# Delta net: first units in the second stage's end, softmax subtraction on GpSimd, z ahead of the first T, tail on two engines

## The reference

```python
x = x + L0_xattn(norm(x), ctx)   # 16 heads over 128 context rows, softmax
x = x + L0_attn(norm(x))         # 16 heads, scores * tril mask, softmax(scores / 8)
x = x + L0_ffn(norm(x))          # Hadamard transforms around a gated MLP of 1024
x = x + L1_xattn(norm(x), ctx)   # 16 heads, causal mask, softmax
x = x + L1_attn(norm(x))         # gated delta net, 16 key heads, 32 value heads
x = x + L1_ffn(norm(x))          # 32 experts, top 8
```

```python
state = state * exp(g_t); delta = (v_t - k_t @ state) * beta_t
state = state + outer(k_t, delta); out_t = q_t @ state
o = out * rsqrt(mean(out**2) + eps) * norm_w * silu(z)     # z: one more projection
```

## Time and profile before

| | us |
|---|---|
| runs shown, median of 3 | 1669.58 (1667.72 to 1670.84) |
| the profiled execution's own time | 1666.14 |
| its span | 1664.3 |
| TensorE busy | 1547.2 (93%) |
| VectorE busy | 1130.2 (68%) |
| ScalarE busy | 598.3 (36%) |
| GpSimd busy | 553.9 (33%) |
| stage 1 | 0 to about 190 |
| stage 2 | about 193 to 520 |
| stage 3 | about 521 to 1398 |
| stage 4 | about 1399 to 1664 |

### The profile page before, as it was taken

One profiled execution on the slowest core, in us unless ns is written; L12 is line 12 of the kernel. 1 busy time (PEld: TensorE's weight loads), 2 busy tenths in 40 slices (PEclk: granted clock), 3 DMA queues, 4 the chain that ended last, 5 costly groups with the idle time before them and its releaser, 6 DMA issues. The chain is left out here.

```text
span 1664.3 us, 34006 instructions
## 1 busy us (share of the span) xinstructions
PE 1547.2 (93%) x14224; PEld 1084.9 (65%) x14224; DVE 1130.2 (68%) x1745; ACT 598.3 (36%) x1038; POOL 553.9 (33%) x885
## 2 busy tenths in 40 slices
PE   7999679979996698999999999999999996999999
PEld 3444358867883366777777777767777784565556
DVE  4666487597675677788888888887788833543433
ACT  2223144345333334444444444444544531111110
POOL 1200052123211545556545465454564431000000
PEclk9999889989998799999999999999999997999999
DMA  7533300010000121121121221112211113200000
GB/s 217 159 90 91 76 1 1 25 28 1 1 1 7 30 42 35 42 56 47 37 52 42 47 50 48 37 46 43 55 46 34 43 27 151 84 1 0 13 1 13
DMA packets 150536, 75.76 MB, mean 46 GB/s; under 512 B 128304, under 2 KB 131632, under 8 KB 148592
## 3 DMA queue, kind: packets, MB, share of 16 engines
q1 hardware_dynamic: 150384, 73.60, 17.5%
HBM read 55.73 MB, written 17.83 MB: 44 GB/s over the span
## 5 line engine op out<-in xcount | busy, mean ns | idle before, releaser
L1719 DVE SCALAR_TENSOR_TENSOR acc<-PS,wc,acc 128x504 f32<-128x504 f32 (+2 forms) x384 | 281.4, 733 | 93.2 <-ACT acc L1452 84.1
L2004 PE MATMUL PS<-HT,wgu 128*128 128x512 f32 x384 | 173.8, 597 | 0.6 <-ACT HT L2050 0.6
L1452 ACT ACTIVATE acc<-PS,wc 128x512 f32<-128x512 f32 x128 | 87.8, 686 | 172.3 <-PE PS L1183 119.7
L1183 PE MATMUL PS<-HT,wv 128*128 128x512 f32 x256 | 128.6, 626 | 11.4 <-DVE acc L1719 11.4
L1729 DVE SCALAR_TENSOR_TENSOR y<-th,acc 128x512 f32<-128x512 f32 x128 | 115.9, 906 | 22.7 <-ACT th L1456 21.4
L1183 PE MATMUL PS<-HT,wkq 128*128 128x512 f32 x256 | 124.5, 610 | 6.6 <-DVE acc L1719 4.7
L1642 POOL TENSOR_TENSOR rr<-nm,con 128x16 f32<-128x16 f32 x16 | 46.8, 2927 | 241.1 <-DVE nm L1747 241.1
L1200 PE MATMUL PS<-wz,HT 128*128 128x256 f32 x512 | 125.1, 392 | 0.7 <-DMA wz<-in_gdn_w 0.7
L2004 PEld LDWEIGHTS PS<-HT,wgu 128*128 128x128 f32 x384 | 73.3, 192 | 74.8 <-issue 72.7
L2140 DVE SCALAR_TENSOR_TENSOR act<-th,PS 128x512 f32<-128x512 f32 x48 | 33.0, 687 | 127.2 <-ACT th L2064 127.2
L1346 PE MATMUL PS<-wo,ogT 128*128 128x256 f32 x512 | 115.3, 383 | 3.5 <-DVE dl L1782 2.4
(11 more groups left out here) (252 smaller groups left out, 3036.5 us busy)
## 6 DMA issues: line engine op xcount, KB each, us to landing
a_rows<-AT SPq DMA_DIRECT2D x16, 512.0 KB, 2.6
wk<-in_l0x_k SPq DMA_DIRECT2D x16, 384.0 KB, 3.6
wgu<-in_moe_gu SPq DMA_DIRECT2D x6, 1024.0 KB, 14.9
queries_scratch<-tts SPq DMA_DIRECT2D x32, 128.0 KB, 2.7
wkq<-in_gdn_w SPq DMA_DIRECT2D x16, 256.0 KB, 2.7
wv<-in_gdn_w SPq DMA_DIRECT2D x16, 256.0 KB, 2.7
wz<-in_gdn_w SPq DMA_DIRECT2D x16, 256.0 KB, 3.3
wo<-in_gdn_w SPq DMA_DIRECT2D x16, 256.0 KB, 3.0
```

The costliest lines, as they stand in the source:

```text
L1183: mm = pe.matmul(PS[:, QB[q], :], w[:, o:o + DK], HT[:, k, f * 512:(f + 1) * 512], start=(k == 0), stop=(k == DC - 1))
L1452: a.activation(acc[:, f, :], PS[:, QB[q], :], ACT.Copy, scale=wc[:, h % 2, 4 * c + 3:4 * c + 4]).then_inc(s["tap"], 1)
L1719: v.scalar_tensor_tensor(a0, p0, wc[:, h % 2, 4 * c + 2 - k:4 * c + 3 - k], a0, ALU.mult, ALU.add).then_inc(s["conv"], 1)
L2004: mm = pe.matmul(PS[:, 2 * (i % 2) + w, :], wgu[:, m, k, w, :], HT[:, k, f * N:(f + 1) * N], start=(k == 0), stop=(k == DC - 1))
```

## The change

1. `w_project`, `w_tap`, `w_tanh`, `w_conv`, `w_silu` and `w_ab` in phase2: the units q = 0, 2, 4 of head 0 (the first 512 tokens of k, q and v0) and the a/b projection of 7 of the 8 tiles are done at the end of stage 2. Their buffers lie over `kvT` and `W2`, which are no longer read then; `y` is now the two halves `yA` and `yB`. phase3 starts its counts at three units and takes the other units in the order 1, 3, 5, 6, 7.
2. The softmax subtraction of parts 1 and 3 moves from VectorE to GpSimd (`lower`). All four orders of phase2 are written anew.
3. phase3's start: a and b are turned into `ga` by GpSimd and VectorE, the z groups of head 0 and a step of its own, `first`, replace `step(0)`; z comes before the first T.
4. `factors`: the power in two halves of 8 columns, the half of k first; the half of q, `sk` and the square of q's half come after `Et`. For all heads.
5. The end of phase3: `sum_o` before `gate`, half of the last multiply and one of the last two copies on VectorE, the norms of phase4's first 4 tiles made around the last residual. The first 1 MB of phase4's weights (`wg0`) is loaded in phase3.

```diff
@@ phase2
-                load(1); load(0); load(2); load(3); load(4); load(5); load(6); load(7)
+                load(0); load(1); load(3); load(2); load(4); load(5); load(6); load(7)
+                def w_project(k):
+                    if k == 0:
+                        pe.wait_ge(s["hT0"], 8)
+                    elif k == 2:
+                        pe.wait_ge(s["w_conv"], 3)
...
+                def w_ab():
+                    for p in range(3):
+                        pe.wait_ge(s[f"hT{p}"], 8)
...
-                turn(4, 3); scores(7, 1); project_out(5, 1); turn_p(6, 1); values(6, 1); project_out(6, 1); turn(5, 3)
-                turn_p(7, 1); turn(6, 3); values(7, 1); project_out(7, 1); turn(7, 3)
...
+                project_out(5, 1); w_project(0); turn_p(6, 1); w_project(1); values(6, 1); w_project(2); project_out(6, 1)
+                turn_p(7, 1); values(7, 1); turn(5, 3); project_out(7, 1); turn(6, 3); w_ab(); turn(7, 3)
...
+                def lower(t, a):
+                    p, n = at(t)
+                    g.wait_ge(s[f"sm{p}"], n * 10 + a * 3 + 6)
+                    g.tensor_tensor(probs(p), probs(p), each(mx[:, p, :], S), ALU.subtract).then_inc(s[f"sm{p}"], 1)
...
-                    v.wait_ge(sem, at0 + 2)
-                    v.tensor_tensor(x, x, each(mx[:, p, :], S), ALU.subtract).then_inc(sem, 1)
...
+                mask_spread(7, 1); residual(5, 3); stats(5, 3); w_conv(0); sums(7, 1); w_conv(1); residual(6, 3)
+                w_silu(0); stats(6, 3); w_silu(1); apply(5, 3); apply(6, 3); w_conv(2); residual(7, 3); stats(7, 3)
+                w_silu(2); apply(7, 3)
@@ phase3, TensorE: the start, and first() in place of step(0)
+                project_ab()
                 project(0, 1)
-                project_ab()
-                for q in range(2, 5):
-                    project(0, q)
+                project(0, 3)
+                project(0, 5)
+                decay_sums(0)
                 scores(0)
-                decay_sums(0)
-                for q in range(5, NQ):
-                    project(0, q)
+                project(0, 6)
+                project_z(0, 0)
+                project(0, 7)
+                project_z(0, 1)
                 turn_v(0, 0)
+                def first():
+                    project(1, 0)
+                    turn_v(0, 1)
+                    project(1, 1)
+                    project_z(0, 2)
+                    decay_sums(1)
+                    project(1, 2)
+                    project_z(0, 3)
+                    project(1, 3)
+                    project(1, 4)
+                    cross(0, 4)
+                    scores(1)
+                    grow(0, 4)
+                    project(1, 5)
...
@@ phase3, GpSimd: factors
+                    g.tensor_tensor(rr[:, par, kh], nm[:, kh], C("mhalf")[:, kh], ALU.pow).then_inc(s["rr"], 1)
...
                         g.tensor_tensor(Et[:, hv, :, :], Ed[:, hv, :, :], over(C("upper"), TILES), ALU.mult).then_inc(s["et"], 1)
+                    g.tensor_tensor(rr[:, par, qh], nm[:, qh], C("mhalf")[:, qh], ALU.pow).then_inc(s["rr"], 1)
+                    g.tensor_tensor(sk[:, par, :], nm[:, kh], rr[:, par, kh], ALU.mult).then_inc(s["rr"], 1)
...
@@ phase3, ScalarE: swap_scale
-                    a.wait_ge(s["rr"], h * 5 + 3)
+                    a.wait_ge(s["rr"], h * 7 + 6)
@@ phase3, SyncE
-                sp.wait_ge(s["pj"], 4)
+                sp.wait_ge(s["pj"], 5)
...
+                sp.dma_start(wg0[:, :, :, :, :], d["moe_gu"][:, 0:PIECE, :, :, :]).then_inc(s["gin"], 16)
@@ phase3, VectorE: last() and behind it
-                    gates(j, False)
+                    for hv in range(2):
+                        v.wait_ge(s["us"], j * 2 + hv + 1)
...
+                        sum_o(hv)
+                    level(j)
+                    for hv in range(2):
+                        gate(hv)
+                    v.wait_ge(s["fz"], j * 2 + 2)
+                    v.wait_ge(s["gz"], j * 2 + 2)
+                    v.tensor_tensor(dl[:, 1, :, :], dl[:, 1, :, :], each(ms[:, 1, :], DK), ALU.mult).then_inc(s["og1"], 1)
                     residual(g, 1)
...
+                keep_second_out()
                 residual(LAST, 0)
...
+                for t in range(4):
+                    stats(t)
...
                 residual(LAST, 1)
+                v.wait_ge(s["nrt"], 1)
+                for t in range(4):
+                    v.tensor_scalar(hn[:, t, :], X[:, t, :], mv[:, t, 0:1], rstd[:, t, :], ALU.subtract, ALU.mult)
```

More of the change, by code:

```diff
@@ L469, in _, with phase2 @@
                         latent(u - 1)
-def phase2(nc, d, sb, semaphores, C, over, each, X, HT, PS, carrier, bn, mv, ve, rstd, hn, kvr, kvT, ctT, TTd, W2, weights):
+def phase2(nc, d, sb, semaphores, C, over, each, X, HT, PS, carrier, bn, mv, ve, rstd, hn, kvr, kvT, ctT, TTd, W2, weights, early, yA, acc, th):
     SLOTS = 4
@@ L974, in _ @@
-                residual(7, 2); stats(7, 2); sums(5, 1); apply(7, 2); key_blocks(6, 1); residual(4, 3); stats(4, 3)
-                mask_spread(6, 1); apply(4, 3); key_blocks(7, 1); sums(6, 1); mask_spread(7, 1); residual(5, 3)
-                stats(5, 3); sums(7, 1); apply(5, 3); residual(6, 3); stats(6, 3); apply(6, 3); residual(7, 3)
-                stats(7, 3); apply(7, 3)
-def phase3(nc, d, sb, semaphores, C, over, each, X, HT, PS, carrier, early):
+                spread_x(0, 0); sums_x(0, 0); spread_x(0, 1); spread_x(1, 0); sums_x(0, 1); spread_x(1, 1); sums_x(1, 0)
@@ L1154, in _ @@
                 sp.sem_inc(s["cin"], 32)
-                sp.wait_ge(s["pj"], 4)
+                for name in ("pj", "tap", "th", "y"):
+                    sp.sem_inc(s[name], AHEAD)
+                sp.sem_inc(s["conv"], 3 * AHEAD)
+                sp.wait_ge(s["pj"], 5)
                 load_kq(1)
@@ L1433, in last @@
                     project_out(g, 3)
-                for j in range(LAST):
+                first()
+                for j in range(1, LAST):
                     step(j)
@@ new lines, in _, with first @@
+                conv(0, 7)
+                silu_z(0, 1)
+                silu(0, 7)
+                def first():
+                    conv(1, 0)
+                    conv(1, 1)
+                    silu(1, 0)
+                    silu_z(0, 2)
+                    conv(1, 2)
+                    silu(1, 1)
+                    silu_z(0, 3)
+                    conv(1, 3)
+                    silu(1, 2)
+                    silu(1, 3)
+                    conv(1, 4)
+                    norms(1)
+                    update(0, 4)
+                    silu(1, 4)
+                    conv(1, 5)
+                    silu(1, 5)
+                    make_A(1, 0)
+                    make_A(1, 1)
+                    update(0, 5)
+                    conv(1, 6)
+                    silu(1, 6)
+                    make_P(1, 0)
+                    make_P(1, 1)
+                    for hv in range(2):
+                        keep_M(0, hv)
+                    conv(1, 7)
+                    silu(1, 7)
+                    gates(0, False)
@@ L2153, in residual @@
                     v.tensor_tensor(x, x, acc(t)[:, 0:D], ALU.add).then_inc(s["res"], 1)
-                for t in range(HALF):
-                    stats(0, t)
-                variance(0)
-                for t in range(HALF):
-                    apply(0, t)
                 for i in range(STREAM):
```

518 lines of the change are left out of this document (321 added, 197 removed).

## The result

| | time, us (median, lowest to highest) | profiled execution | ratio to before, 95% interval |
|---|---|---|---|
| before | 1669.2 (1667.7 to 1670.8) | 1666.14, span 1664.3 | |
| changed | 1650.3 (1649.7 to 1651.6) | 1650.12, span 1648.1 | 0.9887 [0.9871, 0.9903] |

The change makes the kernel 18.9 us faster. The forecast was 1637, in a range from 1620 to 1654: right sign, inside the range, and 13 us more of a gain than came. The two profiled executions differ by 16.0, where the forecast's sum has 32.3; the other 2.9 of the median's gain are not in them, because the profiled execution of before was a short one and that of the changed kernel was not.

The account below looks back on a forecast made before the run. TensorE was taken to bound stage 3's middle, with losses where it waits for other engines. Terms -23 - 12 + 7 - 4.3 = -32.3 took the profiled 1666.14 us to 1633.8, a median of 1637; range 1620 to 1654.

Parts of the forecast that it names:

- Stage 2: Whole of stage 2: subtractions leave VectorE, new orders and added units fill TensorE's holes; -12 us (+6 to -24).
- the head: Start of stage 2: tile 0 finished first, the 5.16 us wait down to about 2.3; -4 us (0 to -7).
- the term of 6: Stage 2, 340 to 376 us: the 4.82 us wait and most slow clock behind it go; -6 us (+2 to -12).
- The start: Stage 3 from its first matmul: head 0's scores and T come earlier; -23 us (-15 to -27).
- the 39.5 us from T to the mark: Stage 3's start, first product with T to step 1's 3.53 us wait: 39.5 us instead of 48.45, 8.9 gained.
- The term of 2 for the low clock: Stage 3's start: 2 us taken off the 24.9 gained, for TensorE's lower clock around its idle time ahead of T.
- The steady steps: Steps 1 to 14 of stage 3: later sk delays ScalarE, TensorE stands about 0.5 us each; +7 us (-1 to +9).
- Rival 1: Stage 3's steady steps have no new wait, because ScalarE's place does not bind; 1630 us, chance 0.15.
- The end: End of stage 3: earlier last projection, norms beside it, stage 4's first transpose earlier; -4.3 us (-2.5 to -5.5).
- Rival 3: Stage 2: GpSimd becomes the bound of the softmax chains, 2.7 us for each of 16; 1692 us in full, chance 0.05.
- Rival 2: Stage 2 gains nothing: added matmuls on TensorE, GpSimd's shares behind other tiles' subtractions; 1649 us, chance 0.17.
- rival 4: Stage 3's start: head 0 gains half, since its a/b part starts late, T 8 us earlier; 1645 us, chance 0.11.

Follow-up runs that it names:

- e5: Changed kernel with the second scaling of the down weights on GpSimd moved behind the third and fourth cross-attention shares in stage 2's head; 1646.3 us, ratio 0.9872.
- the second trace: Trace of the changed kernel measured once more with no edit; median 1650.1 us, ratio 0.9885.
- e6: Changed kernel with three VectorE places moved in stage 3's start: a/b reciprocal, head 1's A halves and unit 6's convolution earlier; 1647.1 us, ratio 0.9869.
- e10: Changed kernel with 7 idle 128x512 matmuls on TensorE ahead of the first product with T; 1646.2 us, ratio 0.9845.
- e3: Changed kernel with the small product sk computed on GpSimd ahead of the two Et products, not behind the second power; 1646.2 us, ratio 0.9848.
- e4: Changed kernel with the 1 MB load of stage 4's first weights issued later, behind step 2's DMAs; 1654.2 us, ratio 0.9898.
- e1: Changed kernel with the 16 softmax subtractions of stage 2 back on VectorE, all orders kept; 1658.4 us, ratio 0.9935.
- e7: Changed kernel with 14 idle 128x512 matmuls on TensorE ahead of the first product with T; 1645.9 us, ratio 0.9856.
- e8: Changed kernel with e3, e5, e6 and, at stage 3's end, ScalarE's last copy ahead of its last output-weight scaling; 1636.9 us, ratio 0.9812.
- e11: Changed kernel with all edits of e8 and the 7 idle matmuls of e10; 1637.1 us, ratio 0.9791.

## Why the prediction was right in sign and 13 us off

**Stage 2, the largest miss (forecast -12, measured -2.9).** The step that failed is the head: "VectorE has no idle time up to its first mask" was true (15.8 and 15.7 us of 16), but what filled it was counted too low. I wrote of some 3 collisions with GpSimd of 1 us each "I count none, since four tiles are under way". In the head four tiles are not enough: VectorE is the bound, and what holds it reaches TensorE. The groups of VectorE in stage 2 of the changed kernel, against a mean of 425 ns for the 32 applies of before, and 4.1 us for the two subtractions of the fold:

```profile
L957 DVE TENSOR_SCALAR hn<-X,mv,rstd 128x256 f32<-128x256 f32 x32 | 17.8, 556 | 12.2 <-POOL rstd L884 12.2
...
L913 DVE TENSOR_TENSOR b<-b 128x1024 f32<-128x1024 f32 x2 | 5.8, 2918 | 0.0
```

That is 4.2 + 1.7 = 5.9 us held, 4.3 of them before 238 us. For the apply e5 shows what it cost; for the 1.7 of the fold no run does. The lock of the port pair (the Trainium skill, SBUF — State Buffer, Who interferes with whom) was the right rule, and I used it for the price of a count of collisions and not for the place of one; there it says that the one who comes second is blocked for the whole of the other's instruction, and the apply's 3.04 us beside a GpSimd instruction of 4.53 agree, as does its 0.41 when that instruction is moved (e5). The wait for the first share fell to 2.18 us as reckoned. At 340 us TensorE had been busy 2.6 us less since 207 than before (120.4 against 123.0), where I had it 4 ahead. The middle came as forecast: from 340 to 376 us it was busy for 32.3 of 36 and not 27.4, all at full clock, which is the term of 6. At the end the units and the a/b part filled holes only in part: TensorE's 40 matmuls for them were busy for 9.1 us, and its idle time from 440 us on fell by 5.5 (12.4 to 6.9). The other 3.6 were paid, less what the higher clock gave there, where I had a gain of 2. The size of the miss is less sure than its place: the second trace has 316.6 us for the stage, 5.6 less than before, and this one 319.3, 2.9 less.

**The start (forecast -23, measured -16.1).** By its own steps: scores at 13.1 behind the first matmul (10.2), norms at 18.9 (16.9), A at 24.6 (22.0), the first product with T at 52.8 (48.9), the mark at 97.2 (88.4, or 90.4 with the 2 for the clock). Two steps failed. The first is the sum of the operations ahead of the scores, 2.9 too low. It lacked that TensorE falls to half clock as it enters the stage (0.61 and 0.53 granted from 518 to 522 us), so that two projections take 5.32 us instead of 3.9 and the first tap comes at 522.2. Behind that tap stand GpSimd's products for the decay sums, which ended last, and VectorE's two gates, which took 2.29 instead of 1.4 beside those products and ended 0.5 us ahead of the scores.

```profile
529.99 1.12 PE L1302 MATMUL PS<-gm,con 128*128 128x512 f32 x2 [0.34 <-POOL gm L1852]
531.04 0.69 PE L1314 MATMUL PS<-kvT 128*64 128x64 f32 x16
```

The first decay sum came at 10.5 and not 8.3. From the scores to the norms it took 5.9, 0.8 less than I had, and another 0.8 falls when the reciprocal of 1.74 us goes where VectorE is idle (e6). From the norms to A it took 0.5 more (the first power took 1.98 and not 1.64) and from A to T 1.4 more, half of it a longer copy of A (3.4 and not 2.6). The second failed step is the 39.5 us from T to the mark, which took 44.4 and which I summed from TensorE's own work. TensorE waits there, 3.11 us at the end, and what ends last is a chain through VectorE, SyncE and GpSimd: T, the scores of head 1, its norms, A, the copy of A, its rows, the substitution, the gates of head 0. From A to the mark it took 27.3 us (587.93 to 615.21) and 24.6 before: 0.9 of the difference is the clearing of T, which the change puts ahead of the gates, and 1.8 the copy of A. Both experiments that shorten this chain, e6 and e10, bring the mark 3 us nearer: 2.4 and 2.0 of it are there at A, the rest comes with a shorter copy. The term of 2 for the low clock was of the right size: from T to A of head 1 it costs 1.3 (e10), on top of what it costs ahead of the scores.

**The steady steps (forecast +7, measured +5.6).** The mechanism is as written: ScalarE's copy of sk is released by GpSimd, 0.49 us late, and TensorE stands for it. The size was off by a fifth: a period of 50.93 instead of 50.54, 0.39 in each step and not 0.5, with the 8-column power, interpolated at 1.64, measured at 1.66:

```profile
L1790 POOL TENSOR_TENSOR rr<-nm,con 128x8 f32<-128x8 f32 x16 | 26.5, 1658 | 233.6 <-DVE nm L1919 233.6
```

Rival 1 (no new wait) falls, and e3 gives the whole of it back, by the period.

**The end (forecast -4.3, measured -2.3).** GpSimd's power starts 2.3 us earlier as reckoned (5.9 behind the output product, 8.2 before), but the first turn only 1.1 (12.3 instead of 13.4): GpSimd's half multiply took 2.93 beside VectorE's half, where one of the two before took 1.88. The last projection starts at 16.9 us behind the output product instead of 18.4: a gain of 1.5 and not 1.95. I had not looked at ScalarE's order: its scaling of the last output weights stands ahead of the copy and waits for their load, which goes out only when the two projections before it are over. These start at 7.0 instead of 4.4, since the gates that they wait for stand behind the sums now (5.05 of wait and not 2.39), and took 5.41 us at a granted clock of 0.72 (1364 to 1370 us) instead of 3.72. The last projection took 8.86 instead of 7.17, at a granted clock of 0.66 (1374 to 1379 us), which took back 1.7; its end had been taken as given. The norms moved beside it as forecast: from its end to the transpose 3.95 us against 6.44.

**The rest.** The load of 1 MB at 0 was right (e4). The 3.4 us between the profiled execution and the median of before were added to the forecast, and the changed kernel's own profile had 0.2: a term of sampling, not of the chip. It hid 3 us of the miss by luck: between the profiled executions 32.3 were forecast and 16.0 came, so the parts together were twice too large. Rival 3 lost its condition, TensorE hardly waited for GpSimd in the chains of the masks (0.55 us in all stage 2). Rival 2 (1649, stage 2 gains nothing) and rival 4 (1645, T comes 8 and not 16 earlier) were each nearer to the time than the forecast, and each has a part of what happened: 9 of the 12 us of stage 2 and 4 of the 16 of T did not come.

**The copy of A for head 1**, 512 KB to DRAM, takes 4.0 to 4.9 us in the changed kernel (both traces), e1, e3, e4 and e5, and 2.7 to 3.3 in e6, e7, e8, e10 and e11. It is not the load of 1 MB (e4). The DMA packets of the traces tell the two apart: in the six slow ones one packet of 16 KB of the queue for instructions begins 0.9 to 2.4 us behind the copy's issue, and 2 to 8 of the copy's 128 large packets end behind it and later than 2.4 us, when all packets of a short copy have ended. In e6, e7, e8 and e10 it lies ahead of the copy's packets or behind them; in e11 (3.3) it begins at 2.8, just as they end. From the first to the last packet of the copy, in the changed kernel and in e7 (queue, kind: packets, MB, share of 16 engines):

```profile
q1 hardware_dynamic: 144, 0.52, 36.0%
q8 instruction: 1, 0.02, 1.5%
```

```profile
q1 hardware_dynamic: 144, 0.52, 66.9%
```

Of the 208 copies of A in the 13 traces, 12 took over 3.3 us, and each of them has such a packet, of 16 or 8 KB, within its first 2.4 us; 2.6 us is the usual time. No run moved such a packet by itself, so this is a coincidence found in every case and not an experiment. If it is the cause, 1.8 us of the second failed step, and what e6 and e10 gained behind A, depend on where the loading of the program happens to fall, which every edit moves.

## What to carry to other kernels

Moving work from VectorE to GpSimd is paid for at places, not on average: list VectorE's instructions that the other can hold, and keep GpSimd's longest ones away from those in a stretch where VectorE is full. A new start, or a new order, should be summed along the chain that ends last and not along TensorE's work, even when TensorE is the bound everywhere else; where it waits twice in 45 us it isn't. When an instruction sequence is cut in two, look at every reader of what now comes second: one product of 0.2 us in the wrong half cost 4 us.

## What the runs showed of the hardware

- A matmul of 128x512 with the identity as the standing operand shows as two passes and takes 0.87 us at full clock (14 in 12.18 us, 7 in 6.17).
- Idle matmuls ahead of a wait keep the clock: with 14 back to back TensorE stayed at 1.00 (2.4 GHz) through the product with T, and with 7 and a gap of 0.9 us the product still took 2.05; without them the granted clock was 0.50 (1.2 GHz) behind the idle stretch, and the product took 3.62.
- A DMA of 512 KB took 2.6 us, and 4.0 to 4.9 where a packet of 16 KB of the instruction queue lay in its first 2.4 us (six traces); that the packet is the cause was not tested by itself.
- VectorE and GpSimd hold each other in turn: a GpSimd share starts 0.16 us behind VectorE's addition of two SBUF operands and takes 2.76 instead of 1.90, and VectorE's subtraction (128x1024, 1.22 alone), which starts while the share runs, takes 2.92 and ends 1.1 us behind it. The rows, from the changed kernel's head of stage 2:

```profile
213.69 1.90 POOL L869 TENSOR_TENSOR b<-b,rs 128x1024 f32<-128x1024 f32 x1 [5.84 <-DVE rs L932]
...
217.28 1.17 DVE L912 TENSOR_TENSOR b<-b 128x1024 f32<-128x1024 f32 x1
217.44 2.76 POOL L869 TENSOR_TENSOR b<-b,rs 128x1024 f32<-128x1024 f32 x1 [1.85 <-DVE rs L932]
218.37 2.92 DVE L913 TENSOR_TENSOR b<-b 128x1024 f32<-128x1024 f32 x1
```
